# Cross attention on one core: other orders in the first batch, at batch ends, at the beginning and in the last body, and 26 matmuls without a reader

## The reference

```
a = layernorm(ctx) * gamma + beta
Q = x @ Wq.T ; K = a @ Wk.T ; V = a @ Wv.T        # 16 heads of 64
S = Q K^T / 8, masked rows of ctx set to -inf
out = softmax(S) V, heads put side by side, then @ Wo.T
y = x + tanh(gate) * out
```

## Time and profile before

| | |
|---|---|
| Timed runs | 2000.68, 2000.82, 2000.74 us; median 2000.74 |
| Profiled execution | 2003.15 us, its span 2001.3 us |
| Granted clock of PE, mean | 0.995 of full speed |
| Busy in the span | PE 1955.9, DVE 1610.2, POOL 1464.8, ACT 1346.3 us |
| Instructions | 26441, of which PE 8720 matmuls |
| DMA | 342 MB, mean 171 GB/s |

### The profile page before, as it was taken

One profiled execution on the slowest core, in us unless ns is written; L12 is line 12 of the kernel. 1 busy time (PEld: TensorE's weight loads), 2 busy tenths in 40 slices (PEclk: granted clock), 3 DMA queues, 4 the chain that ended last, 5 costly groups with the idle time before them and its releaser, 6 DMA issues.

```text
span 2001.3 us, 26441 instructions
## 1 busy us (share of the span) xinstructions
PE 1955.9 (98%) x8720; PEld 1590.8 (79%) x8720; DVE 1610.2 (80%) x2078; ACT 1346.3 (67%) x2438; POOL 1464.8 (73%) x806
## 2 busy tenths in 40 slices
PE   6999999999999999999999999999999999999997
PEld 4777778888788888888888888888888888788886
DVE  6588778888788877888788887888878888778878
ACT  5768876568755686656865678665876568756554
POOL 4899996767866788666877669757696667966664
PEclk8999999999999999999999999999999999999999
DMA  6576544654355443554445543455534644435422
GB/s 232 190 250 243 198 163 168 220 193 139 128 178 197 168 164 124 212 186 146 159 136 206 191 158 120 171 191 180 181 119 139 241 156 155 149 128 191 158 99 106
DMA packets 136502, 341.96 MB, mean 171 GB/s; under 512 B 55856, under 2 KB 56880, under 8 KB 135472
## 3 DMA queue, kind: packets, MB, share of 16 engines
q1 hardware_dynamic: 136368, 340.28, 48.5%
HBM read 288.86 MB, written 51.36 MB: 170 GB/s over the span
## 4 chain that ended last, share of the span: by engine, by line
PE 85%; ACT 6%; DVE 4%; POOL 2%; issue 2%; DMA 1%; SPq 0%; ACTq 0%; DVEq 0%; POOLq 0%
PE pj L439 16%; PE pj L443 16%; PE pj L441 15%; PE sc L393 5%; PE sc L367 5%; PE sc L397 5%; PE sc L368 5%; PE sc L394 5%; PE pv L387 5%; PE pv L388 5%; DVE mq L820 2%; PE pj L376 1%; ACT cx L682 1%; ACT prob L614 1%; ACT x_hi L678 1%
## 5 line engine op out<-in xcount | busy, mean ns | idle before, releaser
L1097 POOL TENSOR_TENSOR p_lo<-prob,p_hi 128x1024 fp32r<-128x1024 f32 x256 | 613.9, 2409 | 183.2 <-ACT p_hi L619 183.2
L439 PE MATMUL pj<-a_hi,w_hi 128*128 128x512 f32 x1024 | 403.6, 394 | 3.5 <-DVE a_lo L909 1.1
L443 PE MATMUL pj<-a_hi,w_lo 128*128 128x512 f32 x1024 | 400.5, 391 | 0.0
L441 PE MATMUL pj<-a_lo,w_hi 128*128 128x512 f32 x1024 | 400.1, 391 | 0.0
L820 DVE TRANSPOSE_TENSOR_REDUCE mq<-sc 128x32 f32<-128x1024 f32 x256 | 304.4, 1227 | 89.3 <-PE sc L368 88.4
L887 DVE SCALAR_TENSOR_TENSOR xy<-sc,tg_b,xy 128x1024 f32<-128x1024 f32 x244 | 305.9, 1272 | 30.4 <-PE sc L397 24.5
L614 ACT ACTIVATE prob<-prob 128x1024 f32<-128x1024 f32 x256 | 271.3, 1060 | 87.2 <-DVE prob L842 86.8
L842 DVE TENSOR_TENSOR prob<-sc,m_b 128x1024 f32<-128x1024 f32 x256 | 301.5, 1219 | 4.4
L1101 POOL TENSOR_TENSOR prob<-prob 128x1024 f32<-128x1024 f32 x126 | 302.3, 2399 | 0.0
L1108 POOL TENSOR_TENSOR r_b<-o,r_b 128x512 f32<-128x512 f32 x62 | 81.1, 1308 | 271.6 <-DVE r_b L859 271.6
L619 ACT CAST p_hi<-prob 128x1024 fp32r<-128x1024 f32 x256 | 269.4, 1053 | 3.5
(11 more groups left out here) (126 smaller groups left out, 3725.0 us busy)
## 6 DMA issues: line engine op xcount, KB each, us to landing
w_hi<-kept_hi SPq DMA_DIRECT2D x225, 512.0 KB, 3.7
w_lo<-kept_lo SPq DMA_DIRECT2D x225, 512.0 KB, 4.6
xy<-in_xT SPq DMA_DIRECT2D x32, 512.0 KB, 6.4
cx<-in_ctx SPq DMA_DIRECT2D x32, 512.0 KB, 7.5
kept_hi<-w_hi SPq DMA_DIRECT2D x32, 512.0 KB, 5.4
kept_lo<-w_lo SPq DMA_DIRECT2D x32, 512.0 KB, 6.2
out_y<-xy SPq DMA_DIRECT2D x7, 2048.0 KB, 9.8
w_raw<-in_wq SPq DMA_DIRECT2D x8, 512.0 KB, 5.3
```

The source lines that it names most:

```text
L439: pe.matmul(dst, w_hi[:, w, cols], s_hi[:, i], start=i == 0, stop=False)
L441: pe.matmul(dst, w_hi[:, w, cols], s_lo[:, i], start=False, stop=False)
L443: mm = pe.matmul(dst, w_lo[:, w, cols], s_hi[:, i], start=False, stop=i == KT - 1)
L1097: pool.tensor_tensor(p_lo[:, 2 * i:2 * i + 2], prob[:, h, 2 * i:2 * i + 2], f32(p_hi[:, 2 * i:2 * i + 2]), ALU.subtract).then_inc(pl_done, 1)
```

## The change

- **Beginning.** POOL does `first_norm` between the two `deviations`, and starts its weight splits only when all four blocks are normalised. DVE, not ACT, writes the first mask rows. ACT copies Q before it makes WK's hi part, makes WV's behind a_float 3, WQ's (pair 1) ahead of the K copies and WK's (pair 1) right behind them. ACT makes a_hi of tiles 2 and 5 only; DVE of the other six. PE does 14 matmuls whose result nobody reads behind the first Q, then turns four tiles instead of three ahead of K, and does V of pair 0 right behind K.
- **First batch.** The split of WO for pair k - 2 moves on ACT from the end of body k - 1 to the start of body k, behind `copy_vt` and `o_high`, and on POOL behind `o_low`. `copy_vt` is the first thing of every body.
- **Batch ends.** In "prepare" bodies a_float of tiles 6 and 7 goes ahead of the second k_high and p_high.
- **Last body.** PE does 12 matmuls without a reader behind `turn_v`. The last p_lo is halved: block 2 on POOL, block 3 on DVE behind `scale`. The output quarters are finished in the order 0, 2, 3, 1 (before: 0, 2, 1, 3), pair 62's product for quarter 3 is added to pair 61's in PSUM, so that one `gather` falls away, and quarter 1 is gathered in two halves.

```diff
-FIRST_HIGH = range(1, KT, 2)
+FIRST_HIGH = (2, 5)
...
+        def out_split(k):
+            b, j = divmod(k - 1, PAIRS)
+            return b, WO, j - 1
...
-                for count, n in enumerate((0, 2, 1, 3)):
-                    sp.wait_ge(acc_done, 4 * LAST + count - (2 if n == 3 else 3))
+                for count, n in enumerate((0, 2, 3, 1)):
+                    sp.wait_ge(acc_done, 4 * LAST + count - (3 if n == 1 else 4))
...
                     scores(k, h, kind)
-                    if k == 0 and h == 0:
-                        take(first, 3 * KT)
...
                 turn_v(k)
+                keep_warm(pj[1], 12)
                 scores(k, 1, "last")
...
                 pe.wait_ge(acc_done, 4 * k - 6)
-                out_pair(k - 2, 3, lower)
+                out_pair(k - 2, 3, lower, done=False)
+                pe.wait_ge(plv_done, 1)
                 values(k, 1, 1)
...
                 before_pair(2, pj_both)
+                before_pair(3, lower, first=False)
                 pe.wait_ge(w_in_last, 32)
                 pe.wait_ge(oh_done, k + 1)
                 last_pair(0, upper)
                 last_pair(2, pj_both)
+                last_pair(3, lower)
                 pe.wait_ge(acc_done, 4 * k - 4)
-                before_pair(1, lower)
-                last_pair(1, lower)
-                pe.wait_ge(acc_done, 4 * k - 3)
-                before_pair(3, upper)
-                last_pair(3, upper)
+                before_pair(1, upper)
+                last_pair(1, upper)
+
+            def keep_warm(dst, n):
+                for _ in range(n):
+                    pe.matmul(dst, x_hi[:, 0, :P], x_hi[:, 1], start=True, stop=True)
 
             first = projections(-1, -1, "switch")
             take(first, 3 * KT)
+            keep_warm(pv[0][:, 0], 14)
             pe.wait_ge(ident_done, 2)
-            for i in range(3):
+            for i in range(4):
                 turn_ctx(-1, -1, i)
...
+            take(first, 3 * KT)
             pe.wait_ge(at_done, KT)
...
             def body(k, b, j, kind):                      # ACT
-                if begun:
-                    copy_vt(k)
+                copy_vt(k)
                 if not (isinstance(k, int) and k < 2):
                     o_high(k - 2)
+                if begun and splits(*out_split(k)):
+                    ge(act, op_done, k * 4 - 8)
+                    split_w(*out_split(k))
...
                 exp(k, 1, 1)
-                k_high(k, 1)
-                p_high(k, 1, 1)
                 if kind == "prepare":
                     a_float(b, 6)
                     a_float(b, 7)
-                if splits(b, WO, j - 1):
-                    ge(act, op_done, k * 4 - 4)
-                    split_w(b, WO, j - 1)
+                k_high(k, 1)
+                p_high(k, 1, 1)
...
+            q_high(-1, 0)
+            q_high(-1, 1)
             act.wait_ge(w_ld[1], 16)
             act.copy(w_hi[:, WK], w_raw[:, 1]).then_inc(whi_done, 1)
...
+                if i == 3:                                # in the loop of a_float
+                    act.wait_ge(w_ld[0], 32)
+                    act.copy(w_hi[:, WV], w_raw[:, 0]).then_inc(whi_done, 1)
...
                 scale(k - 1, o32[:], r_b[:])              # DVE
+                dve.wait_ge(ph_done, k * 4 + 4)
+                dve.tensor_tensor(p_lo[:, 3], prob[:, 1, 3], f32(p_hi[:, 3]), ALU.subtract).then_inc(plv_done, 1)
                 gather(4 * k - 6, lower, 1)
...
+            dve.wait_ge(mask_ld, 16)
+            dve.wait_ge(init_done, 5)
+            for h, row in ((0, HD), (1, 0)):
+                dve.tensor_scalar(kt[row:row + 1, h, 1], mask_u8[row:row + 1], -MASKED, MASKED, ALU.mult,
+                                  ALU.add).then_inc(mrow_done, 1)
             q_low(-1, 0)
...
                 p_low(k, 1, 1)                            # POOL
-                split_w(b, WO, j - 1)
                 if begun:
                     o_low(k - 1)
+                split_w(*out_split(k + 1))
                 key_sums(k, 1)
...
             deviations(-1, 0)
+            first_norm()
             deviations(-1, 1)
-            first_norm()
+            pool.wait_ge(z_done, TB)
             for one in FIRST_SPLITS[1:]:
```

More of the change, by code:

```diff
@@ L110, in xattn_kernel @@
         ones_done, psum_done, pinv_done = sem("ones_done"), sem("psum_done"), sem("pinv_done")
-        prow_done = sem("prow_done")
+        prow_done, plv_done = sem("prow_done"), sem("plv_done")
         y_st, rd_done, rx_done = sem("y_st"), sem("rd_done"), sem("rx_done")
@@ L397, in out_block, with out_pair @@
                 return pe.matmul(dst, w_hi[:, slot, cols], lo, start=False, stop=done)
-            def out_pair(q, n, dst):
+            def out_pair(q, n, dst, done=True):
                 for c in range(2):
-                    mm = out_block(q, WO, 2 * n + c, dst[:, c], o_hi[:], o_lo[:], wait=n == 0 and c == 0)
-                mm.then_inc(op_done, 1)
+                    mm = out_block(q, WO, 2 * n + c, dst[:, c], o_hi[:], o_lo[:], done=done, wait=n == 0 and c == 0)
+                if done:
+                    mm.then_inc(op_done, 1)
             def out_step(k, h, p, kind):
@@ L509, in key_sums, with before_pair @@
                 mm.then_inc(psum_done, 1)
-            def before_pair(n, dst):
+            def before_pair(n, dst, first=True):
                 for c in range(2):
-                    out_block(LAST - 1, WV, 2 * n + c, dst[:, c], before_hi, before_lo, done=False,
+                    out_block(LAST - 1, WV, 2 * n + c, dst[:, c], before_hi, before_lo, first=first, done=False,
                               wait=n == 0 and c == 0)
@@ L519, in last_pair @@
                                    wait=n == 0 and c == 0)
-                    if n == 3 or c == 1:
+                    if n == 1 or c == 1:
                         mm.then_inc(op_done, 1)
@@ L574, in _ @@
                 take(first, 3)
-                if i + 3 < KT:
-                    turn_ctx(-1, -1, i + 3)
+                if i + 4 < KT:
+                    turn_ctx(-1, -1, i + 4)
+            take(first, 3 * KT)
             pe.wait_ge(at_done, KT)
@@ L705, in body @@
                 hand_out_maxima(k, 0)
[L706 to L710, removed]
                 if kind == "switch":
@@ L802, in _ @@
                     a_high(-1, -1, i)
+                if i == 3:
+                    act.wait_ge(w_ld[0], 32)
+                    act.copy(w_hi[:, WV], w_raw[:, 0]).then_inc(whi_done, 1)
             act.wait_ge(gate_ld, 16)
             act.activation(tg[:], gate_in[:], ACT.Tanh).then_inc(tg_done, 1)
[L805 to L810, removed]
             act.wait_ge(w_ld[1], 32)
@@ L813, in _ @@
             act.copy(w_hi[:, WQ], w_raw[:, 1]).then_inc(whi_done, 1)
+            k_high(-1, 0)
+            k_high(-1, 1)
+            act.wait_ge(w_ld[0], 48)
+            act.wait_ge(w_out[WK], 32)
+            act.copy(w_hi[:, WK], w_raw[:, 0]).then_inc(whi_done, 1)
             run_bodies(body, last_body)
@@ L907, in a_low @@
                     dve.tensor_copy(blocks(a_hi[:, i]), at(i)).then_inc(ahv_done, 1)
-                    dve.wait_ge(ahv_done, i // 2 + 1)
+                    dve.wait_ge(ahv_done, len([n for n in range(i + 1) if n not in FIRST_HIGH]))
                 dve.tensor_tensor(blocks(a_lo[:, i]), at(i), f32(blocks(a_hi[:, i])), ALU.subtract).then_inc(alv_done, 1)
@@ L1043, in last_body @@
                 low(k, last_lo, last_r, last_hi)
[L1044 to L1049, removed]
+                gather(4 * k - 4, upper, 0)
+                gather(4 * k - 3, pj_both, 2)
+                gather(4 * k - 2, lower, 3)
+                gather(4 * k - 1, upper, 1, slice(0, 1))
+                gather(4 * k, upper, 1, slice(1, 2))
             dve.memset(masked[:], MASKED).then_inc(init_done, 1)
@@ L1170, in last_body @@
                 pool.tensor_copy(ones, one_from).then_inc(ones_done, 1)
-                for h in range(2):
-                    for i in range(2):
-                        p_low(k, h, i)
+                p_low(k, 0, 0)
+                p_low(k, 0, 1)
+                p_low(k, 1, 0)
+                pool.wait_ge(ph_done, k * 4 + 4)
+                pool.tensor_tensor(p_lo[:, 2], prob[:, 1, 2], f32(p_hi[:, 2]), ALU.subtract).then_inc(pl_done, 1)
             pool.memset(ident[:], 0.0).then_inc(ident_done, 1)
```

2 lines of the change are left out of this document (removed).

## The result

The changed kernel takes 1996.76 us (median of 18 runs, 1994.56 to 2000.4), the kernel before 2002.88 (18 runs, 2000.15 to 2004.01, among them the three of 2000.7). The ratio is 0.9973, 95% interval 0.9966 to 0.998: 5.4 us, between 4.0 and 6.8. Forecast were 10.85 and a time of 1990.0. The profiled execution took 1996.31 us, its span 1994.1 (2001.3 before) at a mean granted clock of 0.999 (0.995): 7.2 us between the two spans. These are what the rows can be set against. What lies around the span grew with the new start, from 1.8 us (median of the runs of before, e10 and e12) to 2.2 (all others), so some 0.4 of the 7.2 doesn't reach the time of an execution; no run shows where it goes. The medians of the 18 runs each are 6.1 apart.

A forecast was written before the change was run, and what follows sets the result against it. PE was taken as the bound, only its idle and low-clock time savable, with the DVE/POOL port as second limit. 8.6 + 1.85 + 0.6 - 0.2 = 10.85 us gave 1990 us; range 1986.5 to 1997.

The forecast's parts named there:

- Steps (1) to (4): Start, up to K of pair 0: transposes 2.7 us earlier, first K matmul at 24.1, K's end at 34.2, not 36.1.
- the first rival: Last K tile: POOL's split takes the shared port before DVE's last subtraction; total gain 6.8 us, 1994; chance 0.25.
- Step (5): Start, V directly behind K: V ends at 39.7, head 1's scores of pair 0 come at 50.1 instead of 58.68.
- 8.6 us: Start, to head 1's scores of pair 0: the whole gain claimed for the new start.
- 1.85: First batch, WO's split moved behind copy_vt: output step at 107.1, not 108.95; 1.85 us gained, bounds 0 and 5.
- 0.6: Six later batch ends, a_float 6 and 7 moved ahead: 0.1 us gained each, bounds -1.5 and 3.8 together.
- 0.2 lost: Last body, p_lo halved and one gather less: 0.2 us lost, bounds 1.5 gained and 1.6 lost.
- The carried difference of 2.4: Whole kernel: the timed median lay 2.41 us below the profiled execution; carried over, 1992.3 profiled became 1989.9.
- POOL absorbs it: Rival, pair bodies: POOL, nearly always busy, can start no more than 4.3 us earlier, so only that remains; 1996.5; chance 0.12.
- slower: Rival, batch ends and last body: POOL's p_low without slack costs 9.5 us together; 2003.8; chance 0.05.
- The clock falls anyway: Rival, 2.5 us idle before K of pair 0: clock stays low into V, up to 3 us lost; 1993; chance 0.11.

The follow-up runs named there:

- e10: Changed kernel with its whole start put back as before, the other edits kept: 2000.3 us, ratio to the kernel before 0.9985.
- e12: Kernel before with matmuls without a reader (11, 9 and 12) in three of its pauses, nothing moved: 1999.4 us, ratio to before 0.9984.
- e1: Changed kernel with V's high and low parts split ahead of the first subtractions in body 0: 1995.3 us, ratio to before 0.9969.
- e2: Changed kernel with nine more matmuls without a reader ahead of K of pair 1: 1994.9 us, ratio to before 0.9964.
- e11: Changed kernel with V's split early, the last body's gather ahead of DVE's p_lo half, and q_low of head 1 earlier in pair 0: 1994.5 us.
- e14: Changed kernel with V's split early, the last body's gather moved ahead, and six matmuls without a reader in each of two waits: 1995.2 us.
- e5: Changed kernel with only the split of WO at its old place: 1996.6 us, ratio to before 0.9975.
- e7: Changed kernel with the gather of output quarter 1 ahead of DVE's half of p_lo in the last body: 1995.2 us, ratio to before 0.9965.
- e3: Changed kernel with V of pair 0 back behind the first scores: 1997.5 us, ratio to before 0.9978.
- e9: Changed kernel without the 12 matmuls in the last body's pause: 1996.7 us, ratio to before 0.9972.
- e4: Changed kernel without the 14 matmuls behind the first Q: 1995.3 us, ratio to before 0.997.
- e13: Changed kernel with nine matmuls ahead of K of pair 1 and the last body's gather ahead of DVE's p_lo half: 1993.9 us, ratio 0.9957.

## Why the forecast was wrong, by its own steps

**The sum of the profile.** 7.2 us of span against 10.85. At the first scores of pair 1 the change leads by 5.35, between pairs 2 and 3 it gains 1.63, over pairs 8 to 62 0.39, and in the last body it loses 0.12. Of the 7.2 some 0.4 falls away around the span.

**Steps (1) to (4): right.** Transposes at 19.87 (19.9), first K matmul at 24.05 (24.1). DVE's last a_lo started at 31.93 and POOL's split at 32.21, so the first rival, the lock at the last K tile, did not occur. POOL came 0.3 us too late for it here, and 0.3 to 0.5 in the ten other kernels with the new start. K ended at 33.5 (34.2), and V was done at 38.93 (39.7).

**Step (5), "Scores 1.8, 36 matmuls 8.2 and the v transposes 0.4 put head 1's scores at 50.1": this failed.** From 38.93 that sum gives 49.3; 53.22 was measured. The 36 matmuls are Q and K of pair 1, and K needs the bank out of which V's parts are read. The step listed k_high, k_low, the splits and copy_vt under V, but not v_high and v_low, which must lie between V and K. They cost 2.04 us of waiting (e1) and, where the clock falls behind it, 1.5 to 1.6 more (e2).

**"8.6 us" as a gain that lasts: wrong also without that wait.** e1, e11 and e14 put head 1 at 49.3 to 49.7, earlier than forecast, and pair 1 at 63.0 to 63.5, where e2, e5 and e7, with the wait and no fall of the clock, have 63.4 to 63.7. The limit there is DVE's queue behind head 1's scores: PE waits 1.51 for q_low in e1, and 2.23 for k_low in e11, where q_low is early. So of the 8.6 us no order tried here kept more than 7.4 (70.46 less 63.02) to pair 1. Against e12 the orders of the start are worth 67.80 - 63.5 = 4.3 us: 1.2 of it is V's place (e3 has 64.67), 3.1 the rest of the new start. The other 2.66 is the low clock that they avoid.

**Which part was clock.** The start's 5.35 is 2.66 of before's low clock, 4.3 of orders, less 1.6 of the new low stretch. In the whole span, fillers in the kernel before bring 3.9, the orders from there to e2 4.9, and the new stretch costs 1.6: 7.2. These are differences of single profiles.

**First batch, "1.85": near, and mostly for the reason named.** 1.63 was measured, all of it clock (e5, e12). The forecast had 1.6 of clock and only 0.25 of the shorter wait in it, since it let the output step wait for the subtraction; by e5 the 0.25 is nothing. That the shorter wait is what held the clock isn't shown: in e5 the clock held behind the longer one. The two vt waits that it counted at nothing went from 1.56 and 1.54 to 0.6 each, and the waits for the output step grew to 1.2, as it said.

**Batch ends, "0.6":** 0.4, and the cx wait is gone, with nine waits for a_lo of up to 0.3 behind the ends (1.9 in all). The last four of the six batches are 0.14 to 0.18 shorter each, the first two 0.06 and 0.24 longer. With the old start (e10) all six are shorter, by 1.2 together.

**Last body, "0.2 lost":** 0.12 lost. The gather behind DVE's half was named as the thing that PE waits for, and e7 confirms it: turned round, it is 1.5 gained.

**The carried difference of 2.4.** The three runs of before that the forecast went by, 2000.7, lie at the fast end of 2000.2 to 2004.0. The profiled 2003.15 was near the median of all. From the profile alone the forecast would have been 1992.3.

**"POOL absorbs it" and "slower" did not occur.** From pair 3 to pair 8 the changed kernel took 163.07 us and the one before 163.04, so the lead passed through the rest of the first batch whole; and over the six later batch ends, where "slower" had its losses, 0.39 was gained.

**"The clock falls anyway"** cost time at a place that the rival did not name, K of pair 1. At the place that it did name, K of pair 0, the clock fell in six of the eleven kernels with the new start, though not in the changed one, and the answer given against it held: e5's first scores came no later. The forecast took each stretch of low clock as a fixed cost of its pause. It isn't: behind V's wait of 2.04 us the clock fell in the changed kernel and in e9, and not in e4, e5 and e7.

## What to carry to other kernels

When work of PE is moved ahead, list for each bank that it writes who must read it before the next writer comes, and where those reads stand in their engines' queues. Split a measured stretch into idle time and low clock before counting it as the price of an order: matmuls without a reader in the pauses of the old kernel tell the one from the other, and here they brought 3.5 us by themselves, more than half of what the whole change did. Where the clock falls only in some executions, one profile of each kernel can mislead by the price of a stretch: compare profiles that have the same low stretches. A lead at one point is not yet a gain; ask what the other engines would allow at the next.

## What the runs showed of the hardware

- The clock falls behind the same idle stretch in some profiles and not in others, each of another kernel. Behind 2.04 us: two of five (the changed kernel and e9; not e4, e5 and e7). Behind 2.14 in pair 2: in the kernel before, not in e5. Behind 2.1 to 2.4 us ahead of K of pair 0: six of eleven. In the last body, behind a wait for p_lo of 1.07 in e3 and 1.09 in e13, and in none of the other ten kernels with the 12 matmuls, which have waits of 0.7 and 1.1 there too. The Trainium skill, "TensorE: Matmul & The Clock Gate", section "Part 1: The HAM clock gate", says that the point where the clock rises varies from run to run; here the fall differs too, over profiles of different kernels. The timed runs fit to that: of the changed kernel's 18, two with a mean granted clock of 0.997 took 1999.4 us on average, ten with 0.999 took 1996.4 and two with 1.000 took 1995.3. The spread is 5.8 us over the changed kernel's runs, 1.3 for e12 (11 runs) and e13 (5) with their fillers.
- One such stretch costs what PE can't hide: 2.66 in pair 0 before, 1.6 in pair 2, 1.5 behind V's wait, 1.3 in e11 (first scores of pair 1 to head 1's, 16.3 instead of 15.0), 0.1 to 0.4 in the last body.
- A DVE operation with two SBUF inputs is held up beside POOL: the half of p_lo took 1.78 us beside POOL's half and 0.68 behind it, while the gather, which reads PSUM, took 1.27 in both orders.
